# A two-layer block on one Trainium2 core: the first down-weight butterflies on GpSimd instead of VectorE

## What is computed

```python
xn = layernorm(x)                                  # x: 8 chunks of 512 tokens, 512 features
s = linear_attention(xn)                           # phi(k)*v, running sum over tokens, times phi(q), then Wo
h = fwht(xn * SU_ug) / 64                          # fwht: normalised Walsh-Hadamard transform
h = silu(h @ W_gate.T * c_gate) * (h @ W_up.T * c_up)       # 2048 hidden features
g = silu((fwht(h * SU_dp) / 64) @ W_down.T * c_down)
out = x + s * g
```

## Time and profile before

| | us |
|---|---|
| runs of before (three) | 1316.66, 1317.06, 1319.61; median 1317.06 |
| profiled execution | 1318.89 |
| its span | 1317.1 |
| PE busy in the span | 1284.1 (97%) |
| DVE busy | 868.9 (66%) |
| ACT busy | 541.6 (41%) |
| GpSimd busy | 63.3 (5%) |

### The profile page before, as it was taken

The page is one execution under the profiler, slowest core; times in us unless marked ns, Lnnn a source line. Parts: engine busy times, 40 slices in busy tenths (PEclk is TensorE's granted clock), DMA queues, the critical chain, the costliest instruction groups (busy, mean ns, idle before and its releaser), DMA issues.

```text
span 1317.1 us, 15824 instructions
## 1 busy us (share of the span) xinstructions
PE 1284.1 (97%) x6004; PEld 581.6 (44%) x6004; DVE 868.9 (66%) x1335; ACT 541.6 (41%) x819; POOL 63.3 (5%) x108
## 2 busy tenths in 40 slices
PE   5989999999999999999999999999999999999998
PEld 2534444444444444444444444444444444444443
DVE  6989999978866777766715755566643774455422
ACT  4874665540225655541204554442113554443000
POOL 1000111121000010100000000010000000000000
PEclk9999999999999999999999999999999999999999
DMA  9512543568665366634535333334444333323230
GB/s 373 208 64 81 175 163 141 189 235 310 190 259 174 130 218 230 227 127 156 198 124 195 124 105 120 128 131 157 160 165 166 117 109 116 127 100 126 99 125 33
DMA packets 54364, 209.92 MB, mean 159 GB/s; under 512 B 12048, under 2 KB 12304, under 8 KB 37648
## 3 DMA queue, kind: packets, MB, share of 16 engines
q1 hardware_dynamic: 45744, 179.55, 38.4%
q0 software_dynamic: 8544, 29.37, 6.6%
HBM read 163.78 MB, written 45.11 MB: 159 GB/s over the span
## 4 chain that ended last, share of the span: by engine, by line
PE 58%; DVE 2%; issue 2%; ACT 2%; DMA 1%; DVEq 0%; ACTq 0%
PE bank L1639 35%; PE bank L1745 19%; PE bank L1777 5%; DMA h_all<-scr_f 1%; ACT work L809 1%; DVE work L1100 1%; ACT work L812 1%; DVE work L1084 0%; DVE work L1090 0%; ACT work L799 0%; ACT L809 0%; DVE work L1123 0%; DVE h_all L1204 0%; DVE h_all L1205 0%; DVE h_all L1217 0%
## 5 line engine op out<-in xcount | busy, mean ns | idle before, releaser
L1639 PE MATMUL bank<-xops,ring 128*128 128x512 f16 x2772 | 602.5, 379 | 4.9 <-DVE work L1084 2.8
L1639 PEld LDWEIGHTS bank<-xops,ring 128*128 128x128 f16 x2772 | 269.6, 98 | 336.8 <-issue 7.0
L1745 PE MATMUL bank<-h_all,ring 128*128 128x512 f16 x1536 | 333.3, 379 | 1.2 <-DMA ring<-scr_d 1.2
L1084 DVE TENSOR_TENSOR work<-bank,work 128x512 f32<-128x512 f32 x198 | 133.8, 686 | 167.7 <-PE bank L1639 155.1
L1542 PE MATMUL bank<-xops,ring 128*128 128x512 f16 x1008 | 228.4, 381 | 6.0 <-DVE ring L1189 6.0
L1745 PEld LDWEIGHTS bank<-h_all,ring 128*128 128x128 f16 x1536 | 150.2, 98 | 182.7 <-DMA ring<-scr_d 1.7
L799 ACT ACTIVATE work<-bank 128x512 f32<-128x512 f32 x198 | 117.8, 595 | 260.9 <-PE bank L1639 260.2
L1542 PEld LDWEIGHTS bank<-xops,ring 128*128 128x128 f16 x1008 | 98.3, 98 | 130.5 <-issue 10.5
L895 ACT ACTIVATE gates<-bank,d_out 128x512 f32<-128x512 f32 x32 | 19.4, 688 | 220.1 <-PE bank L1745 220.1
L1369 DVE SCALAR_TENSOR_TENSOR x_res<-gates,vec,x_res 128x512 f32<-128x512 f32 x32 | 21.9, 747 | 129.8 <-ACT gates L895 104.7
L829 ACT ACTIVATE h_all<-work 128x512 f16<-128x512 f32 x128 | 77.9, 624 | 65.4 <-DVE work L1123 65.2
(11 more groups left out here) (176 smaller groups left out, 865.0 us busy)
## 6 DMA issues: line engine op xcount, KB each, us to landing
ring<-scr_g SPq DMA_DIRECT2D x66, 1024.0 KB, 4.8
ring<-scr_d SPq DMA_DIRECT2D x32, 1024.0 KB, 5.4
scr_g<-ring SPq DMA_DIRECT2D x22, 512.0 KB, 3.2
h_all<-in_ug_t SPq DMA_DIRECT2D x8, 1024.0 KB, 11.9
x_res<-in_x_t SPq DMA_DIRECT2D x32, 256.0 KB, 4.0
out<-x_res SPq DMA_DIRECT2D x32, 256.0 KB, 6.8
scr_g<-ring POOLq DMA_DIRECT2D x12, 512.0 KB, 4.7
work<-in_x_t SPq DMA_DIRECT2D x6, 1024.0 KB, 7.1
```

The source lines that it names most:

```text
L1084: dve.tensor_tensor(tile(g, j), at[:, :], tile(g, j), ALU.add).then_inc(summed, 1)
L1639: mm = pe.matmul(to[:, :], weight_of(slot, s, b, kk), xops[:, kk, xs, c, :], start=(a == 0 and m in (P1, P2, P5)), stop=(a == 5), skip_gro ...
L1745: mm = pe.matmul(bank[D_BANK[t]][:, :], w[:, t, ws, :], at[:, s, :], start=(a == 0 and b == 0 and n == 0), stop=(a == KB - 1 and b == KB - ...
```

## The change

GpSimd makes all four butterfly levels of block 0, in its program between the spread of the gate and up maxima and the spread of the coefficients' maximum (`first_butterflies`). Blocks 1 to 3 stay on DVE. `scale_down(0)` moves from tile 24 to tile 28 of the DVE program. Level 0 waits for the block's load and for `flown` 2 (the scratch is shared with the first two `fly_rows`); level 1 writes into the raw block and waits for `d_squared` 1; the levels are chained by `first_flown`, and the last counts `d_flown`, which `fold_down(0, 0)` waits for.

```diff
--- before.py
+++ after.py
@@ -85,6 +85,7 @@
 
 DOWN_FROM, DOWN_EVERY = 20, 16
 SCALE_DOWN_AT, FOLD_DOWN_AT, TAKE_DOWN_AT = 4, (7, 9, 11, 13), (9, 11, 13, 14)
+FIRST_SCALE_DOWN_AT = 8
 DOWN_HIGH_AT, DOWN_LOW_AT = 14, 15
 
 
@@ -289,6 +290,7 @@
         fold_done, stage_made = sem("fold_done"), sem("stage_made")
         attn_hi, ug_hi, piece_made = sem("attn_hi"), sem("ug_hi"), sem("piece_made")
         s_summed, s_hi, s_made = sem("s_summed"), sem("s_hi"), sem("s_made")
+        first_flown = sem("first_flown")
         d_squared, d_bounded, d_flown = sem("d_squared"), sem("d_bounded"), sem("d_flown")
         d_folded, d_scaled, d_hi, d_made = sem("d_folded"), sem("d_scaled"), sem("d_hi"), sem("d_made")
         o_max_ready, o_bounded, o_scaled = sem("o_max_ready"), sem("o_bounded"), sem("o_scaled")
@@ -357,6 +359,16 @@
         def flown_low(i, m):
 
             return raw_ug[:, i, m, 0:2, :].rearrange("p k n -> p (k n)").bitcast(F16)
+
+        def butterflies(e, level):
+
+            raw, mid = raw_down(e).rearrange("p (r k) n -> p r k n", r=KB), fly_down
+            src, dst = (mid, raw) if level % 2 else (raw, mid)
+            lows = (slice(0, KB, 2), slice(0, 2))[level % 2]
+            highs = (slice(1, KB, 2), slice(2, KB))[level % 2]
+            if level < 2:
+                return (src[:, :, lows, :], src[:, :, highs, :]), (dst[:, :, lows, :], dst[:, :, highs, :])
+            return (src[:, lows, :, :], src[:, highs, :, :]), (dst[:, lows, :, :], dst[:, highs, :, :])
 
         def made_down(e):
             return ring[:, 3 + e % 2, :].rearrange("p (k s n) -> p k s n", k=NI, s=2)
@@ -642,12 +654,27 @@
                 pool.dma_start(scr_g[n, :, 2048:4096], sum_part(n, 2)) \
                     .then_inc(s_stored if n < S_RING else s_late_stored[n % 2], 16)
 
+            def first_butterflies():
+
+                pool.wait_ge(d_loaded[0], 16)
+                pool.wait_ge(flown, 2)
+                for level in range(4):
+                    if level == 1:
+                        pool.wait_ge(d_squared, 1)
+                    if level:
+                        pool.wait_ge(first_flown, level)
+                    (low, high), (to_low, to_high) = butterflies(0, level)
+                    pool.tensor_tensor(to_low, low, high, ALU.add)
+                    last = pool.tensor_tensor(to_high, low, high, ALU.subtract)
+                    last.then_inc(first_flown if level < 3 else d_flown, 1)
+
             for m in (K, V, Q):
                 pool.wait_ge(attn_squared, m + 1)
                 all_max(m, m + 1).then_inc(attn_bounded, 1)
             load_blocks(0)
             pool.wait_ge(max_ready, 1)
             all_max(M_SU, M_UP + 1).then_inc(max_all_ready, 1)
+            first_butterflies()
             pool.wait_ge(max_ready, 2)
             all_max(M_COEF, M_COEF + 1).then_inc(max_all_ready, 1)
             down_bound(0)
@@ -1287,20 +1314,10 @@
 
             def fly_down_level(e, level):
 
-                raw, mid = raw_down(e).rearrange("p (r k) n -> p r k n", r=KB), fly_down
-                src, dst = (mid, raw) if level % 2 else (raw, mid)
                 if level == 0:
                     dve.wait_ge(d_squared, e + 1)
-                    if e:
-                        dve.wait_ge(d_made, e)
-                lows = (slice(0, KB, 2), slice(0, 2))[level % 2]
-                highs = (slice(1, KB, 2), slice(2, KB))[level % 2]
-                if level < 2:
-                    low, high = (src[:, :, lows, :], src[:, :, highs, :])
-                    to_low, to_high = (dst[:, :, lows, :], dst[:, :, highs, :])
-                else:
-                    low, high = (src[:, lows, :, :], src[:, highs, :, :])
-                    to_low, to_high = (dst[:, lows, :, :], dst[:, highs, :, :])
+                    dve.wait_ge(d_made, e)
+                (low, high), (to_low, to_high) = butterflies(e, level)
                 dve.tensor_tensor(to_low, low, high, ALU.add)
                 last = dve.tensor_tensor(to_high, low, high, ALU.subtract)
                 if level < 3:
@@ -1407,8 +1424,9 @@
                 e, at = down_of(4 * g + part)
                 if e is not None:
                     if at < 4:
-                        fly_down_level(e, at)
-                    elif at == SCALE_DOWN_AT:
+                        if e:
+                            fly_down_level(e, at)
+                    elif at == (SCALE_DOWN_AT if e else FIRST_SCALE_DOWN_AT):
                         scale_down(e)
                     elif at in TAKE_DOWN_AT:
                         take_down(e, TAKE_DOWN_AT.index(at))
```

## The result

The changed kernel takes 1323.81 us (median of 7 runs, 1322.23 to 1326.80) against 1317.06 us (7 runs, 1316.03 to 1320.45): slower, ratio 1.0051 with a 95% interval of 1.0038 to 1.0063, that is 5.0 to 8.3 us. Forecast was 1326.5 with a range of 1310.5 to 1331, and slower as the likeliest. The profiled execution took 1323.29 us, span 1321.3.

A forecast was written before the change was run, and what follows sets the result against it. PE, busy 97%, was taken as the bound, waiting for DVE's `ug_low`. DVE's delay of 13.9 us less 2.28 and 2.26 gave +9.4 on the median 1317.06: 1326.5 us, range 1310.5 to 1331.

The forecast's parts named there:

- Where the time is lost and what relief is worth: PE waits ahead of tiles 24 and 28 plus slow tile 28 cost 7.67 us; relieving DVE alone gains 6.2 us.
- DVE blocked by GpSimd's reads: GpSimd's two-input reads hold the shared SBUF path, so DVE's two-input instructions wait: 18.4 us of blocking; chance 0.54.
- The price of an instruction: Each of GpSimd's eight butterfly instructions takes 2.3 us, twice DVE's; bounds 1.14 and 4.1 us.
- What is absorbed: Of 18.4 us blocking, 2.0 falls into DVE's idle time and 2.5 beside one-input work, L1100 and small instructions.
- L: DVE's delay from GpSimd's blocking, all ahead of piece 6: 18.4 - 2.0 - 2.5 = 13.9 us.
- The sum: L less the relief ahead of piece 6 and the second wait, L - 2.28 - 2.26 = +9.4 us, kept to the end.
- the clock term: Tile 28's matmuls on PE take 4.45 us instead of 2.75 at the slow clock: 1.70 us, left unchanged in the sum.
- Where PE would wait: On PE, a wait of about 15 us ahead of tile 24 and none ahead of tile 28.
- Starving: Rival: DVE keeps the read path, GpSimd finishes only about 113 us, PE waits at the fold; 1321 to 1322.7 us, chance 0.10.
- No blocking: Rival: GpSimd's reads do not hold off DVE, so the whole 6.2 us is gained, 1310.9 us; no or little blocking 0.25.

The follow-up runs named there:

- memsets: Changed kernel with GpSimd's eight adds and subtracts replaced by eight memsets of the same outputs, writing as much and reading nothing: 1310.91 us, ratio 0.9958 to the kernel before.
- the halves: Changed kernel with each of GpSimd's eight instructions cut into two of half the columns, sixteen in all: 1323.68 us, ratio 1.0045 to the kernel before.
- the copies: Changed kernel with GpSimd's eight adds and subtracts replaced by eight copies of one input each: 1318.40 us, ratio 1.0012 to the kernel before.
- the four orders tried first: Kernel before, butterflies on DVE: all turns one tile later 1.0101, two 1.0072; only block 0's levels at tiles 22 to 25 0.9991, at 21, 22, 24, 26 0.9997.
- level 0 alone: GpSimd makes only level 0 of block 0, DVE levels 1 to 3 at their old tiles: 1317.24 us against 1316.46 before, ratio 1.0006.

## Why the prediction was right, point by point

- **Where the time is lost and what relief is worth.** Right. Without butterflies the kernel gained 5.9 us (3.9 to 7.8), forecast 6.2; the wait left was 1.3 us, forecast 1.43. Whether the 1.7 us of the clock belong to it is open.
- **DVE blocked by GpSimd's reads.** Right, and shown: writes cost nothing, one input under half, two inputs 2.07 us per instruction of 1024 columns, half of it for half the columns. Rows 7 and 8 had shown only that GpSimd waits; the rows after show DVE waiting as well. The rule of the Trainium skill (SBUF — State Buffer, Who interferes with whom) that was set beside them in the prediction holds in both directions here (the scan takes 2.59 us beside GpSimd's two-input reads and 1.22 beside its memsets).
- **The price of an instruction.** I took 2.3 us; the hold is 2.07, while an instruction on GpSimd takes 2.35 at the least. Eight holds make 16.6, not 18.4.
- **What is absorbed.** Forecast 2.0 in idle time and 2.5 beside one-input instructions. Measured: the idle times of 1.09 and 0.64 are filled, 1.7, and L1127 takes 0.7 of three holds, 2.1. L is then 16.6 - 1.7 - 2.1 = 12.8; by the start of `ug_low` it is 102.50 + 0.91 - 93.14 + 2.28 = 12.55, forecast 13.9. One reason given was wrong: no small instruction with one SBUF input ran beside GpSimd. In the changed kernel all but one came after it; where they did meet (the halves, the copies), they were held.
- **The sum.** 12.55 - 2.28 - 2.26 = 8.0, against 9.4. What the prediction had wrong beside this size is the clock term, which I left as it is. PE's slow stretches now fell at 82 to 87 us (5.28 us for 12 matmuls) and at 97 to 101 (4.16), both between waits for DVE, where a slower PE only shortens the next wait; tile 28, which was slow and on the path in the profiled execution of before, is at full speed (2.75). Between these two executions 1.7 us came back: 8.0 - 1.7 = 6.3, and 6.15 by the timelines.
- **What the clock term is worth between the medians.** It is not shown that this term belongs in the difference of the medians, 6.75 (5.0 to 8.3), which holds 6.3 and 8.0 alike. The profiled execution of before, 1318.89, is 1.8 us above its median and has two slow stretches that cost time, at 20 us and on tile 28. The profiled execution with the scale's move alone, 1316.43, is a closer twin of the changed one (first spread at 61.41 in both, 4.0 us behind the last matmul in both), and its slow stretch, on tile 24, costs nothing. Against it the changed kernel starts the down product 7.8 us later (296.21 against 288.38), which is the sum without the clock term, and ends its last matmul 6.7 us later; most of the difference is a wait of 1.1 us for DVE at 474 us in the twin, 0.25 in the changed kernel.

The windows show the granted clock of the changed kernel in the two slow stretches and between tiles 24 and 28 (columns as in the earlier trace rows):

```profile
81.00:84.00 3.00, 1.90 (x5) 0.74 (x6) 2.97 (x3) 0.00 (x0) 3.00 (x2) 0.51 0.00 0
...
97.00:101.00 4.00, 4.00 (x12) 1.29 (x12) 3.93 (x6) 1.45 (x2) 1.08 (x2) 0.64 0.00 0
...
107.00:115.00 8.00, 8.00 (x38) 3.73 (x37) 7.90 (x11) 4.06 (x8) 0.00 (x0) 1.00 0.26 103
```

- **Where PE would wait.** Forecast: one wait of 15 us ahead of tile 24. In fact three, 4.07, 3.19 and 2.14 us: the delayed `times_v` held PSUM banks, so PE stopped earlier and had less left to wait for. The start of tile 24 is set by DVE in either case.
- **The rivals.** Starving did not happen: GpSimd's instructions took 2.35 to 3.33 us, alternating with DVE's. No blocking is excluded by the durations. The time alone would not have decided: the starved case was priced at 1321 to 1322.7, 1.1 us from the measured 1323.81, and the range of 1310.5 to 1331 held nearly every case. That the centre came within 2.7 us is in part luck: the price made DVE's delay too long by 1.8 us, and what was to be absorbed made it too short by 0.7.

What stays open: the copies cost more than the stretches explain. Ahead of piece 6 they delay DVE by 4.0 us (its `ug_low` begins at 93.87 against 89.43 with memsets, and the execution started 0.42 later; the stretched instructions there add up to the same 4.0), and PE is 4.3 us later, the 0.42 included, when it starts the down product (287.63 against 283.29). The ratios put some 7 us between the two. In the profiled execution of the copies 5.3 us more arise after that, part of them in waits of PE for the down weights' loads (3.6 us in two waits, 1.4 in one with memsets). Whether the copies cause this was not followed up.

## What to carry to other kernels

Before moving work to GpSimd, add up what DVE does at that time: each GpSimd instruction that reads two SBUF operands takes away from DVE about 2 us per 1024 fp32 columns, here more than the 1.14 us that DVE needs for the same work, so where DVE has no idle time and its own instructions there read two SBUF operands, the move loses even if GpSimd has nothing else to do. What GpSimd could take here at no cost was work that only writes; one level that fell half into DVE's idle time gained and lost nothing. When a busy engine makes others wait, first ask what stands in front of the instruction that is waited for: putting the same eight instructions behind it gained 0.25% where offloading them lost 0.5%, once the chain behind them (folds, takes, the last store) had been followed too; the four orders tried first lost time or gained nothing.

## What was not expected of the hardware

- A change of what GpSimd does, from the spread to adds and subtracts and back, left it idle for 6.9 and 6.0 us with no instruction shown. The memsets followed the spread at once (the spread began at 61.01 and took 0.73, the first memset began at 61.61), and so did the copies (61.43, 62.04), behind the same waits.
- Instructions of DVE on 16 columns or one are held as long as large ones: 1.18 instead of 0.17 us (L981 beside the halves, one SBUF input) and 2.23 instead of 0.13 (L1270). The Trainium skill (SBUF — State Buffer, Who interferes with whom) names `tensor_scalar` among those that can take the shared ports; the trace agrees with 1.18 us against 0.17.
- The slow clock after PE has idled does not always fall on the same tile: before it was tile 28, and in the profiled executions with the scale's move alone and with level 0 alone, which had nearly the same waits up to there (3.71 and 3.54 us), it was tile 24 (4.45 us). One execution of each kernel was profiled, so what decides it is not shown. With the scale's move alone it cost nothing there: the wait ahead of tile 28 shrank from 2.26 to 0.57, and tile 28 began at the same time (107.48 in an execution 0.91 ahead) and ran at full speed. In these traces a slow stretch cost time only where PE, and not DVE, set the pace.
